# The attention score as three fp16 products in place of one fp32 product

## The chip, the cores and the metric

One core of a Trainium2 chip runs the whole program. The metric is the device time of that core in microseconds (us), the median of several runs. A core has TensorE (PE; its weight loads are PEld), VectorE (DVE), ScalarE (ACT), GpSimd (POOL, which does nothing here) and SyncE (SP, which issues the transfers). Each engine works through its own list of instructions in the order written; semaphores tie the lists together.

## The reference, cut to what matters

For 16 batches of 512 tokens with 512 features:

```
h   = gelu(x @ fc1_w.T + fc1_b)                       # 2048 hidden
x2  = x + concat(h @ fc2_w.T + fc2_b, h @ experts_w[idx].T + experts_b[idx])
att = tanh(x2 @ W1 + b1)                              # 128 values for each token
scores = att @ v                                      # one number for each token
out = x2 + softmax(scores under a prefix, postfix or all-but-own mask) @ x2 / count
```

The change touches `scores = att @ v` alone: a product of a 128-vector with a 128 x 512 tile per batch.

## The kernel before, in words

The tokens lie along the free dimension. A batch is one turn of the loop at L530 (82 us). All work of an engine is an order written out by hand, with a semaphore on each edge; nothing is planned by a program except that the VectorE list spreads the small steps of the pooling (`pool(n)`: the next n steps of the generator at L1172) between its other instructions.

**Split products.** Nearly all products are done as three fp16 products of a high and a low part: ScalarE writes the high part (`copy` with a scale, L622 and L623, as in `high`, L649), VectorE the low part (`low_part`, L1061 and L1062: value times scale minus high part), and TensorE adds weight-high x data-high, weight-high x data-low and weight-low x data-high. The scales are powers of two, found from a bound: a column of `mx` is summed over the partitions by TensorE (`chain_sum`, L274), and `chain_scale` (L1016) makes the scale `ex` and its inverse `ix` of it.

**The first layer** of a batch n is done in eight pairs of tiles, p = 0 to 7, by seven half-size products each (Strassen-like: `product1` to `product7`, L318 to L368, six 256-column matmuls each by `six`, L303). Between them VectorE adds halves in PSUM: `add_first` (L1107, its instruction is L1111) must be done before `product7` of that pair, and `add_second` (L1113, L1116) before `product4` and `product3`. ScalarE copies `product1` and `product5` (`copy_first`, `copy_fifth`) and does the gelu. Cycle c of L370 holds `product1(c)`, `product4(c-1)`, `product3(c-1)` and so on in steady order.

**The opening** (L433): at the end of batch b TensorE already starts pairs 0 and 1 of batch n = b + 1, mixed with the last expert products and the last chunk of the attention product, `attend(b, 3)`, whose two fp32 passes are L426. Then ScalarE does `tanh(b)` (L762, L769), from PSUM `pa` into `att`, TensorE does `score(b)` (L428, L431), and ScalarE keeps the result (`keep_score`, L771). The order around it:

```
TensorE  L444-449  attend(b,3) product7(n,0) product5(n,1) product6(n,1) product2(n,1) score(b)
         next      product4(n,0) product3(n,0) product1(n,2) product7(n,1) ...
ScalarE  L807-815  copy_first(n,1) tanh(b) copy_fifth(n,1) keep_score(b)
VectorE  L1453-57  add_first(n,0) add_second(n,0) pool(2) add_first(n,1) pool(3)
         L1393-06  pool(3) add_second(n,1) pool(1) add_first(n,2) low(n,0) pool(1) low(n,1) pool(1) add_second(n,2) ...
```

The stationary operand of the score is `avs`, the vector v repeated in 128 columns, so that every partition gets every score. `product1(n, 2)` writes the bank that holds the score and waits for `scored`. Batch 0 is done with simpler products (`tile`, L288) and a start-up of its own (L475 to L527); VectorE's part of it is L1365 to L1388. The last batch, 15, has its own end (L555 on), with `score_half` (L471) reading `avs` and `att` in two halves.

Of the kernel before, what the change touches and what calls it, by code (L numbers as in the profile page):

```python
# [35 lines left out]
def build(nc, xT, idx, pt, w1, b1, w2, b2, ew, eb, aw, ab, av, iota, ident, tokens, out):  # L36
# [4 lines left out]
    def sb(name, shape, dt=f32):  # L41
        return nc.alloc_sbuf_tensor(name, shape, dt)
# [20 lines left out]
    x2h = nc.alloc_sbuf_tensor_at("x2h", [P, S], f32r, offset=here())  # L63
    fifth = sb("fifth", [P, 2, HALF])
    aws_at = here()
    aws, avs = sb("aws", [P, KD, A]), sb("avs", [A, P])
    early_at = here()
    early = sb("early", [P, A])
    awl = [sb("awl0", [P, A], f32r), sb("awl1", [P, A], f32r),
# [17 lines left out]
    zFi, zFx = zF[:, 1:S + 1], zF[:, 0:S]  # L87
    zBx = zB[:, 1:S + 1]
    io = sb("io", [P, S], f16)
    b1s, b2s, ebs, abs_ = sb("b1s", [P, NH]), sb("b2s", [P, 3]), sb("ebs", [P, 2]), sb("abs", [P, 1])  # L90
    lcol, scol, shift, limit = sb("lcol", [P, 4]), sb("scol", [P, 4]), sb("shift", [P, 4]), sb("limit", [P, B])
    rz, ones = sb("rz", [P, 4]), sb("ones", [P, 1])
    idxs, pts = sb("idxs", [1, B], i32), sb("pts", [P, B], i32)
    ptf, e0, e1, e2 = (early[:, 64 + i * B:64 + (i + 1) * B] for i in range(4))
    cF, cS, cB, cntp, cntq, cD = (sb(n, [P, B]) for n in ("cF", "cS", "cB", "cntp", "cntq", "cD"))
# [1 line left out]


    oneb = sb("oneb", [P, P], bf16)
    NC = 17  # L100
    mx, ex, ix, lift = sb("mx", [P, NC], bf16), sb("ex", [P, NC]), sb("ix", [P, NC]), sb("lift", [P, NC])
    w1c, w2c = 3, 11

    def hc(b):
        return 14 * (b % 2)
# [7 lines left out]
    def scale_of(col):  # L113
        return ix[:, col:col + 1]
# [65 lines left out]
    def sem(name):  # L180
        return nc.alloc_semaphore("s_" + name)

    def sems(name, n):
# [2 lines left out]
                                       sems("ein", 2), sems("ebin", 2))  # L186
    (e0_in, idx_in, pt_in, b1_in, b2_in, aw_in, ab_in, av_in, io_in, eye_in, lcol_in) = (
        sem(n) for n in ("e0in", "idxin", "ptin", "b1in", "b2in", "awin", "abin", "avin", "ioin", "eyein", "lcolin"))

    (bits_set, summed, tile_done, p1, p5, p6, p7, p3, fc2_done, half_done, attended, score_done, nat_done, cols_done,  # L190
     totals_done, piece_done) = (sem(n) for n in (
# [78 lines left out]
    def tensor_program(eng):  # L270
# [3 lines left out]
        def chain_sum(n, lo, hi):  # L274

            if n > 1:
                e.wait_ge(pss_read, n - 1)
            mm(pss[:, lo:hi], oneb[:, :], mx[:, lo:hi], start=True, stop=True).then_inc(summed)
# [147 lines left out]
                mm(pa, aws[:, c, :], chunk(b, c), start=start, stop=stop).then_inc(attended)  # L426

        def score(b):  # L428
            e.wait_ge(tanh_done, b + 1)
            e.wait_ge(av_in, 16)  # L430
            mm(pa, avs[:, :], att, start=True, stop=True).then_inc(score_done)  # L431

        def opening(b):  # L433

# [35 lines left out]

        def score_half(v, n):  # L471
            e.wait_ge(tanh_done, LAST + 1 + v)
            mm(pf[n][:, 0:HALF], avs[:, :], att[:, HALVES[v]], start=True, stop=True).then_inc(score_done)


# [44 lines left out]
        attend(0, 0)  # L520
        fc2(0, 2, range(0, 4))
        e.wait_ge(bound_step, 6)
        chain_sum(9, hc(1), hc(1) + 3)
        fc2(0, 2, range(4, 16))
        attend(0, 1)
        fc2(0, 3, range(0, 12))
# [91 lines left out]
    def scalar_program(eng):  # L618
# [3 lines left out]
        def copy(o, x, scale=1.0):  # L622
            return act(o, x, ACT.Copy, scale=scale)  # L623
# [138 lines left out]
        def tanh(b):  # L762
            e.wait_ge(attended, nth_chunk(b, KD - 1))
            e.wait_ge(ab_in, 16)
            if b:
                e.wait_ge(score_done, b)
            else:
                e.wait_ge(sums_low_done, 2)
            act(att, pa, ACT.Tanh, bias=abs_[:, 0:1]).then_inc(tanh_done)  # L769

        def keep_score(b):  # L771
            e.wait_ge(score_done, b + 1)
            if b:
                e.wait_ge(pool_step, pool_value(b - 1, 11))
            else:
                e.wait_ge(sums_low_done, 1)
            copy(sc, pa).then_inc(scored)

        def exponentials(b, lo):
            e.wait_ge(pool_step, pool_value(b, 12))  # L780
# [91 lines left out]
        seed(0, 3)  # L872
        split_expert_high(0, 0)
        split_expert_high(0, 1)
        split_x_high(1, X11)
        split_x_high(1, T1)
        split_expert_high(0, 2)
# [118 lines left out]
    def vector_program(eng):  # L996
# [19 lines left out]
        def chain_scale(n, lo, hi):  # L1016

            e.wait_ge(summed, n)
            e.wait_ge(ones_set, 7)
            stt(ex[:, lo:hi], pss[:, lo:hi], TINY, lift[:, lo:hi], ALU.max, ALU.mult).then_inc(pss_read)  # L1020
            bits = ex[:, lo:hi].bitcast(i32)
            e.wait_ge(pss_read, n)
            ts(bits, bits, EXPONENT, None, ALU.bitwise_and).then_inc(ex_done)
            e.wait_ge(ex_done, n)
            eng.reciprocal(ix[:, lo:hi], ex[:, lo:hi]).then_inc(ix_done)
# [8 lines left out]
            ts(is2[:, b % 2, lo:hi], ix[:, col:col + hi - lo], ix[:, hc(b):hc(b) + 1], None, ALU.mult).then_inc(ds2_done)  # L1034

        def batch_scales(b):
            chain_scale(8 + b, hc(b), hc(b) + 3)
            fc1_scale(b, 8 + b, 0, PAIRS)
            out_scales(b, 8 + b, 3, 4, ec(b))
            out_scales(b, 8 + b, 0, 3, w2c)  # L1040
# [95 lines left out]
        def sums_low(p):  # L1136
            three, one = raw[:, p * 1024:p * 1024 + 768], raw[:, p * 1024 + 768:p * 1024 + 1024]
            c = scale_of(w1c + p)
            e.wait_ge(ones_high, p + 1)
            low_part(flat(w1l[:, 2 * p + 1, 0:2, :]), one, c, flat(w1h[:, 2 * p + 1, 0:2, :])).then_inc(sums_low_done)  # L1140
            e.wait_ge(three_high, p + 1)
            low_part(flat(cl[:, p, :, :]), three, c, flat(ch[:, p, :, :])).then_inc(sums_low_done)

        def pads():
            eng.memset(mF[:, 0:1], -BIG).then_inc(pads_set)
# [135 lines left out]
        eng.memset(ones[:, :], 1.0).then_inc(ones_set)  # L1281
        eng.memset(oneb[:, :], 1.0).then_inc(ones_set)
        eng.memset(x5[:, :, KD:KD + 1], 1.0).then_inc(ones_set)
        for lo, hi, power in ((0, 2, -14), (2, 11, -12), (11, 16, -14), (16, 17, -12)):
            eng.memset(lift[:, lo:hi], 2.0 ** power).then_inc(ones_set)
        w1_biggest(0)
        e.wait_ge(x_in[0], 16)
# [75 lines left out]
        for q in range(4):  # L1363
            w2_low(2, 0, q)
        weight_sums(0)  # L1365
        bounds(1)
        for p in range(4):
            sums_low(p)
# [2 lines left out]
        combine(1, T1)  # L1371
        combine(1, T2)
        expert_low(0, 1)
        pads()
        masks()
        combine(1, T3)
# [7 lines left out]
        weight_sums(4)  # L1384
        add_first(1, 0)
        add_second(1, 0)
        add_first(1, 1)
        sums_low(4)  # L1388


        for b in range(1, B):

            takes = ((0, 3, 1), (1, 1, 1), (1, 2, 1), (1, 2, 0), (1, 2, 0), (2, 2, 0))  # L1393
            if b == 1:
                takes = ((0, 0, 0),) * 5 + ((1, 1, 1),)
            for c, (one, two, three) in zip(range(2, PAIRS), takes):
                if c > 2:
                    low(b, 2 * c - 6)
                    pool(one)
                    low(b, 2 * c - 5)  # L1400
                pool(two)
                add_second(b, c - 1)
                pool(three)
                add_first(b, c)
                if b == 1 and 3 <= c < 6:
                    sums_low(c + 2)
            low(b, 10)
            pool(2 if b == 1 else 1)
            low(b, 11)
            pool(2 if b == 1 else 1)  # L1410
            add_second(b, PAIRS - 1)
            expert_low(b, 0)
            expert_low(b, 1)
            pool(2)
            low(b, 12)
            low(b, 13)
            expert_low(b, 2)
            expert_low(b, 3)
            low(b, 14)
            low(b, 15)  # L1420
            if b == LAST:
                break

            pool(1 if b == 1 else 2)
            if b == 1:
                for c in range(3):
                    e.wait_ge(awl_high, c + 1)
                    tt(awl[c][:, :], aws[:, c, :], awl[c][:, :].bitcast(f32), ALU.subtract).then_inc(awl_low)
            pool(3 if b == 1 else 4)
            bounds(b + 1)  # L1430
            pool(0 if b == 1 else 2)
            batch_scales(b + 1)
            for t in (T1, T2, T3, T4):
                combine(b + 1, t)
            pool(3)
            x2_low(b, 0)
            x_low(b + 1, X11)
            x_low(b + 1, T1)
            x_low(b + 1, T2)
            pool(3)  # L1440
            x_low(b + 1, X21)
            pool(2)
            x2_low(b, 1)
            x_low(b + 1, T3)
            x_low(b + 1, X22)
            pool(3)
            x_low(b + 1, T4)
            pool(3)
            x2_low(b, 2)
            pool(1)  # L1450
            pool(4)
            pool(3)
            add_first(b + 1, 0)  # L1453
            add_second(b + 1, 0)
            pool(2)
            add_first(b + 1, 1)
            pool(3)
# [70 lines left out]
    def sync_program(eng):  # L1528
# [35 lines left out]
        dma(b2s[:, :], b2).then_inc(b2_in, 16)  # L1564
        dma(pts[:, :], pt).then_inc(pt_in, 16)
        dma(abs_[:, :], ab).then_inc(ab_in, 16)
        dma(avs[:, :], av).then_inc(av_in, 16)
        dma(io[:, :], iota).then_inc(io_in, 16)
        dma(lcol[:, :], tokens).then_inc(lcol_in, 16)
        dma(aws[:, :, :], aw).then_inc(aw_in, 16)  # L1570
# [12 lines left out]
        for b in range(1, B):  # L1583
            if b < LAST:
                load_expert(b + 1)
            else:
                e.wait_ge(attended, nth_chunk(LAST - 1, 2))
                dma(aws[:, 0:3, :], aw[:, 0:3, :]).then_inc(aw_in, 16)
            if b > 1:
                for c in (1, 2, 3):  # L1590
                    store(b - 2, c)
            if b == LAST:
                e.wait_ge(el_done, nth_chunk(LAST, 3))
                dma(eye, ident).then_inc(eye_in, 16)
            store(b - 1, 0)
# [61 lines left out]
```

## Time and profile before

| | |
|---|---|
| time, median of 3 runs | 1362.59 us (1361.64 to 1362.98) |
| the profiled execution: its time | 1362.06 us |
| the profiled execution: its span, first to last instruction | 1360.3 us |
| busy in that span | TensorE 1348.4 us, VectorE 1231.0 us, ScalarE 868.7 us |
| mean granted TensorE clock | 0.999 of full speed |

The times in the rows are microseconds from the span's start; a duration without a unit is in us, "mean ns" is in nanoseconds. "Idle before" is the time in which the engine stood still ahead of these instructions, with what ended it. Matmuls are pipelined, so the distance between the starts of two of them, and not the duration of one, is what one costs in a stream.

### The profile page before, as it was taken

To read this page: it belongs to the slowest core of one execution; us is meant where nothing else is said; L and a number is where in the kernel's file an instruction comes from. 1 tells how busy PE (TensorE), PEld (TensorE's weight loads), DVE (VectorE), ACT (ScalarE), POOL (GpSimd) and SP (SyncE) were. 2 spreads that over 40 slices of the span, in tenths; PEclk is the share of its full clock that TensorE was granted. 3 is DMA by queue.
4 is the path that set the end of the run, shared out by engine and by line. 5 is a ranking of instruction groups with operands and counts; after the bars stand their busy time and mean duration, and the time that the engine had idled before them with its cause. 6 is when DMAs were issued, how large, how long until landed. Compare 5 with 4: busy or idle time off the path is not lost.

```text
span 1360.3 us, 22015 instructions
## 1 busy us (share of the span) xinstructions
PE 1348.4 (99%) x8734; PEld 869.8 (64%) x8734; DVE 1231.0 (90%) x2057; ACT 868.7 (64%) x1493; POOL 0.2 (0%) x4
## 2 busy tenths in 40 slices
PE   9999999999999999999999999999999999999998
PEld 4348476584766748567584765848567584765856
DVE  7896889899898998989899898998989999898998
ACT  4867848477583756838477483766838468483753
POOL 0000000000000000000000000000000000000000
PEclk9999999999999999999999999999999999999999
DMA  8410011110201102011020201102011020200001
GB/s 292 149 37 33 1 63 32 39 56 1 78 17 55 40 1 78 16 63 32 19 76 1 71 25 47 48 0 78 17 62 32 9 78 9 66 29 14 25 10 55
DMA packets 29192, 62.98 MB, mean 46 GB/s; under 512 B 5922, under 2 KB 6690, under 8 KB 26658
## 3 DMA queue, kind: packets, MB, share of 16 engines
q1 hardware_dynamic: 28658, 61.05, 13.8%
q8 instruction: 69, 1.13, 0.4%
q10 hardware_dynamic: 432, 0.53, 0.1%
q14 instruction: 33, 0.27, 0.1%
HBM read 44.79 MB, written 16.78 MB: 45 GB/s over the span
## 4 chain that ended last, share of the span: by engine, by line
PE 90%; DVE 7%; ACT 2%; DMA 1%; issue 0%; ACTq 0%; DVEq 0%
PE ps L394 14%; PE ps L396 14%; PE ps L395 14%; PE ps L313 13%; PE ps L314 13%; PE ps L315 13%; PE ps L284 1%; PE ps L431 1%; PE ps L426 1%; PE ps L596 1%; PE ps L422 1%; PE ps L421 1%; PE ps L420 1%; DVE hl L1062 1%; DMA er<-in_w 1%; DVE mx L1001 0%
## 5 line engine op out<-in xcount | busy, mean ns | idle before, releaser
L394 PE MATMUL ps<-hh,w2l 128*128 128x512 f16 x768 | 291.3, 379 | 0.7 <-ACT ps L623 0.7
L396 PE MATMUL ps<-hl,w2h 128*128 128x512 f16 x768 | 291.2, 379 | 0.0
L395 PE MATMUL ps<-hh,w2h 128*128 128x512 f16 x768 | 291.2, 379 | 0.0
L313 PE MATMUL ps<-xh,w1h 128*128 128x256 f16 x960 | 261.8, 273 | 0.0
L314 PE MATMUL ps<-xl,w1h 128*128 128x256 f16 x960 | 261.8, 273 | 0.0
L315 PE MATMUL ps<-xh,w1l 128*128 128x256 f16 x960 | 261.8, 273 | 0.0
L647 ACT ACTIVATE g<-ps,b1s,ds 128x512 f32<-128x512 f32 x240 | 173.5, 773 | 99.5 <-PE ps L315 98.5
L313 PE MATMUL ps<-xh,ch 128*128 128x256 f16 x720 | 196.4, 273 | 0.6 <-ACT ps L623 0.3
L315 PE MATMUL ps<-xh,cl 128*128 128x256 f16 x720 | 196.3, 273 | 0.0
L314 PE MATMUL ps<-xl,ch 128*128 128x256 f16 x720 | 196.3, 273 | 0.0
L1062 DVE SCALAR_TENSOR_TENSOR hl<-g,ix,hh 128x512 f16<-128x512 f32 x244 | 177.3, 739 | 1.6
L623 ACT ACTIVATE hh<-g,ix 128x512 f16<-128x512 f32 x244 | 162.1, 718 | 0.0
L396 PEld LDWEIGHTS ps<-hl,w2h 128*128 128x128 f16 x768 | 75.0, 98 | 90.8
L623 ACT ACTIVATE ps<-ps 128x256 f32<-128x256 f32 x120 | 44.6, 372 | 138.0 <-PE ps L315 138.0
L394 PEld LDWEIGHTS ps<-hh,w2l 128*128 128x128 f16 x768 | 74.9, 98 | 90.0 <-issue 4.3
L395 PEld LDWEIGHTS ps<-hh,w2h 128*128 128x128 f16 x768 | 75.0, 98 | 81.2 <-issue 0.7
L314 PEld LDWEIGHTS ps<-xl,w1h 128*128 128x128 f16 x960 | 93.8, 98 | 22.2 <-issue 5.0
L313 PEld LDWEIGHTS ps<-xh,w1h 128*128 128x128 f16 x960 | 93.9, 98 | 20.8 <-issue 3.6
L315 PEld LDWEIGHTS ps<-xh,w1l 128*128 128x128 f16 x960 | 93.9, 98 | 10.9
L394 PE MATMUL ps<-hh,el 128*128 128x512 f16 x240 | 91.3, 381 | 0.0
L395 PE MATMUL ps<-hh,eh 128*128 128x512 f16 x240 | 91.0, 379 | 0.0
L396 PE MATMUL ps<-hl,eh 128*128 128x512 f16 x240 | 91.0, 379 | 0.0
(208 smaller groups left out, 2343.3 us busy)
## 6 DMA issues: line engine op xcount, KB each, us to landing
xr<-in_xT SPq DMA_DIRECT2D x62, 256.0 KB, 3.1
er<-in_ew SPq DMA_DIRECT2D x15, 1024.0 KB, 5.6
out<-xr SPq DMA_DIRECT2D x60, 256.0 KB, 2.4
raw<-in_w SPq DMA_DIRECT2D x28, 256.0 KB, 6.2
er<-in_w SPq DMA_DIRECT2D x3, 1024.0 KB, 10.1
xr<-in_ew SPq DMA_DIRECT2D x1, 1024.0 KB, 5.7
out<-er SPq DMA_DIRECT2D x3, 256.0 KB, 2.5
xr<-in_xT ACTq DMA_DIRECT2D x2, 256.0 KB, 5.1
```

What stands on the lines that cost most here:

```text
L284: m = mm(pf[k % 4], w1r[k][:, c * P:(c + 1) * P], xr[:, 0, c, :], start=c == 0, stop=c == KD - 1)
L313: mm(to, wh, mh, start=i in (1, 5) and c == 0, stop=False, skip_group_check=True)
L314: mm(to, wh, ml, start=False, stop=False, skip_group_check=True)
L315: m = mm(to, wl, mh, start=False, stop=c == 1, skip_group_check=True)
L394: mm(po(b, o), wl, hh[:, k, :], start=False, stop=False, skip_group_check=True)
L395: mm(po(b, o), wh, hh[:, k, :], start=False, stop=False, skip_group_check=True)
L396: m = mm(po(b, o), wh, hl[:, k, :], start=False, stop=k == NH - 1, skip_group_check=True)
L420: mm(pa, awl[c][:, :], x2h[:, :], start=start, stop=False)
L421: mm(pa, awh[:, c, :], x2l[:, :], start=False, stop=False)
L623: return act(o, x, ACT.Copy, scale=scale)
L647: act(in_two(g_of(b, k)), src, ACT.Gelu, bias=b1s[:, k:k + 1], scale=ds1[:, b % 2, p:p + 1]).then_inc(gelu_done)
L1062: return stt(o, src, scale, hi, ALU.mult, ALU.subtract)
```

## The change

Batches 0 to 14 get their score from three fp16 products. `tanh` stays; ScalarE then copies `att` times 2^13 into `hh[:, 0, :]` (the slot of the hidden tile 0, which has been read by then) as fp16, and VectorE writes the low part into `hl[:, 0, :]` (`attention_low`). The vector v is loaded as one column (`vcol`), gets a scale like the weights (a new column `vc` = 17 of `mx`, `ex`, `ix`, summed along with the scales of batch 1), and `vh`, `vl` are its fp16 parts, repeated over 128 columns, in the place of `avs`. `keep_score` multiplies by `vinv`, which takes the scales out again. Batch 15 keeps the fp32 product; `avs` is loaded for it late.

```diff
@@ TensorE
         def score(b):
-            e.wait_ge(tanh_done, b + 1)
-            e.wait_ge(av_in, 16)
-            mm(pa, avs[:, :], att, start=True, stop=True).then_inc(score_done)
+            e.wait_ge(atth_done, b + 1)
+            e.wait_ge(vl_done, 1)
+            mm(pa, vl[:, :], hh[:, 0, :], start=True, stop=False)
+            mm(pa, vh[:, :], hh[:, 0, :], start=False, stop=False)
+            e.wait_ge(attl_done, b + 1)
+            mm(pa, vh[:, :], hl[:, 0, :], start=False, stop=True).then_inc(score_done)
...
         e.wait_ge(bound_step, 6)
-        chain_sum(9, hc(1), hc(1) + 3)
+        e.wait_ge(vmax_done, 1)
+        chain_sum(9, hc(1), vc + 1)
@@ ScalarE
             act(att, pa, ACT.Tanh, bias=abs_[:, 0:1]).then_inc(tanh_done)
+            e.wait_ge(tanh_done, b + 1)
+            copy(hh[:, 0, :], att, grow[:, 0:1]).then_inc(atth_done)
...
-            copy(sc, pa).then_inc(scored)
+            e.wait_ge(vinv_done, 1)
+            copy(sc, pa, vinv[:, 0:1]).then_inc(scored)
...
         split_expert_high(0, 1)
+        e.wait_ge(ix_done, 9)
+        copy(vh[:, :], vcol.broadcast_to([A, P]), scale_of(vc)).then_inc(vh_done)
         split_x_high(1, X11)
@@ VectorE
+        def attention_low(b):
+            e.wait_ge(atth_done, b + 1)
+            low_part(hl[:, 0, :], att, grow[:, 0:1], hh[:, 0, :]).then_inc(attl_done)
...
+        eng.memset(grow[:, :], 2.0 ** 13).then_inc(ones_set)
...
         weight_sums(0)
+        e.wait_ge(vcol_in, 16)
+        column(vc, vcol[:, :]).then_inc(vmax_done)
         bounds(1)
...
         expert_low(0, 1)
+        e.wait_ge(vh_done, 1)
+        low_part(vl[:, :], vcol.broadcast_to([A, P]), scale_of(vc), vh[:, :]).then_inc(vl_done)
+        ts(vinv[:, :], ex[:, vc:vc + 1], 2.0 ** -13, None, ALU.mult).then_inc(vinv_done)
         pads()
...
         add_second(1, 0)
+        attention_low(0)
         add_first(1, 1)
...
             add_second(b + 1, 0)
+            attention_low(b)
             pool(2)
             add_first(b + 1, 1)
@@ SyncE
-        dma(avs[:, :], av).then_inc(av_in, 16)
+        dma(vcol[:, :], av[:, 0:1], allow_slow_non_contiguous=True).then_inc(vcol_in, 16)
...
                 dma(aws[:, 0:3, :], aw[:, 0:3, :]).then_inc(aw_in, 16)
+                e.wait_ge(score_done, LAST)
+                dma(avs[:, :], av).then_inc(av_in, 16)
```

Beside this, the scales of batch 1 are taken over four columns in place of three, the small per-partition columns (`ones`, `abs_`, `rz`) move into one tile with the new ones, and `score_half` waits for `av_in`.

## Rows read from the trace of the kernel before

**Rows 1.** The page: busy time, and the chain that ended last, by engine.
```profile
PE 1348.4 (99%) x8734; PEld 869.8 (64%) x8734; DVE 1231.0 (90%) x2057; ACT 868.7 (64%) x1493; POOL 0.2 (0%) x4
...
PE 90%; DVE 7%; ACT 2%; DMA 1%; issue 0%; ACTq 0%; DVEq 0%
```

**Rows 2.** Timeline of TensorE, batch 4: start, duration, engine, line, operation, names.
```profile
428.75 0.38 PE L396 MATMUL ps<-hl,eh 128*128 128x512 f16 x1
428.97 0.38 PE L394 MATMUL ps<-hh,el 128*128 128x512 f16 x1
...
435.72 1.02 PE L431 MATMUL ps<-raw,avs 128*128 128x512 f32 x2
...
436.58 0.27 PE L313 MATMUL ps<-xh,w1h 128*128 128x256 f16 x1
```

**Rows 3.** Timeline of ScalarE in the same opening: tanh.
```profile
433.30 0.69 ACT L769 ACTIVATE raw<-ps,abs 128x512 f32<-128x512 f32 x1 [0.49 <-PE ps L426]
```

**Rows 4.** ScalarE by groups: mean ns of one, with and without a scale.
```profile
L623 ACT ACTIVATE hh<-g,ix 128x512 f16<-128x512 f32 x244 | 162.1, 718 | 0.0
L623 ACT ACTIVATE x2h<-xr 128x512 fp32r<-128x512 f32 x42 | 26.5, 631 | 58.1 <-PE ps L422 57.9
```

**Rows 5.** Timeline of VectorE, batch 4 to 5: first scan of the opening, add_second of pairs 1, 4, 6.
```profile
434.30 1.21 DVE L1253 TENSOR_TENSOR_SCAN raw<-raw 128x512 f32<-128x512 f32 x1
...
440.59 0.42 DVE L1116 TENSOR_TENSOR ps<-ps,fifth 128x256 f32<-128x256 f32 x1
...
441.86 0.74 DVE L1062 SCALAR_TENSOR_TENSOR hl<-g,ix,hh 128x512 f16<-128x512 f32 x1
442.51 1.22 DVE L1253 TENSOR_TENSOR_SCAN raw<-raw 128x512 f32<-128x512 f32 x1
...
454.73 0.41 DVE L1116 TENSOR_TENSOR ps<-ps,fifth 128x256 f32<-128x256 f32 x1
...
463.94 0.40 DVE L1116 TENSOR_TENSOR ps<-ps,fifth 128x256 f32<-128x256 f32 x1
```

**Rows 6.** Timeline of TensorE: the first matmul of product4 of pairs 1, 4, 6.
```profile
441.84 0.27 PE L313 MATMUL ps<-xh,w1h 128*128 128x256 f16 x1
...
455.60 0.27 PE L313 MATMUL ps<-xh,w1h 128*128 128x256 f16 x1
...
464.76 0.27 PE L313 MATMUL ps<-xh,w1h 128*128 128x256 f16 x1
```

**Rows 7.** Waits of VectorE, 434.2 to 480 us: us in total, times, longest.
```profile
DVE el L1062 <- ACT eh L623: 1.9, 2, 1.3
```

**Rows 8.** Timeline: TensorE held back by an add, and ScalarE by itself.
```profile
103.98 0.43 DVE L1111 TENSOR_TENSOR ps<-ps,fifth 128x256 f32<-128x256 f32 x1
104.55 0.27 PE L313 MATMUL ps<-xh,ch 128*128 128x256 f16 x1 [0.30 <-DVE ps L1111]
...
1315.12 0.72 ACT L947 ACTIVATE xr<-io,shift 128x512 f32<-128x512 f16 x1 [4.38 <-DVE shift L1481]
1315.88 0.72 ACT L949 ACTIVATE xr<-xr,limit 128x512 f32<-128x512 f32 x1
```

**Rows 9.** Timeline of the start-up and of the first opening.
```profile
79.84 0.47 DVE L1062 SCALAR_TENSOR_TENSOR w1l<-raw,ix,w1h 128x256 f16<-128x256 f32 x1
...
86.28 0.75 DVE L1062 SCALAR_TENSOR_TENSOR el<-xr,ix,eh 128x512 f16<-128x512 f32 x1 [0.72 <-ACT eh L623]
...
93.10 0.75 DVE L1062 SCALAR_TENSOR_TENSOR el<-xr,ix,eh 128x512 f16<-128x512 f32 x1
...
93.90 0.39 PE L394 MATMUL ps<-hh,el 128*128 128x512 f16 x1
...
106.71 0.43 DVE L1111 TENSOR_TENSOR ps<-ps,fifth 128x256 f32<-128x256 f32 x1 [0.88 <-PE ps L315]
```

**Rows 10.** The score's matmuls, first and last start; SyncE's timeline behind the last.
```profile
L431 PE MATMUL ps<-raw,avs x30: 592/594/595, 107.2 to 1256.4; 128*128 128x512 f32 x30
...
1260.35 23.14 SPq L1554 DMA_DIRECT2D out<-xr  x3
```

More of the change, by code:

```diff
@@ L65, in build @@
     aws_at = here()
-    aws, avs = sb("aws", [P, KD, A]), sb("avs", [A, P])
+    aws, avs_at = sb("aws", [P, KD, A]), here()
+    avs = sb("avs", [A, P])
+    vh, vl = (nc.alloc_sbuf_tensor_at(n, [A, P], f16, offset=avs_at + at) for n, at in (("vh", 0), ("vl", 2 * P)))
+    cols = sb("cols", [P, 16])
+    ones, abs_, vcol, vinv, grow, rz = (cols[:, lo:hi] for lo, hi in ((0, 1), (1, 2), (2, 3), (3, 4), (4, 5), (8, 12)))
     early_at = here()
@@ L89, in build @@
     io = sb("io", [P, S], f16)
-    b1s, b2s, ebs, abs_ = sb("b1s", [P, NH]), sb("b2s", [P, 3]), sb("ebs", [P, 2]), sb("abs", [P, 1])
+    b1s, b2s, ebs = sb("b1s", [P, NH]), sb("b2s", [P, 3]), sb("ebs", [P, 2])
     lcol, scol, shift, limit = sb("lcol", [P, 4]), sb("scol", [P, 4]), sb("shift", [P, 4]), sb("limit", [P, B])
-    rz, ones = sb("rz", [P, 4]), sb("ones", [P, 1])
     idxs, pts = sb("idxs", [1, B], i32), sb("pts", [P, B], i32)
@@ L99, in build @@
     oneb = sb("oneb", [P, P], bf16)
-    NC = 17
+    NC = 18
     mx, ex, ix, lift = sb("mx", [P, NC], bf16), sb("ex", [P, NC]), sb("ix", [P, NC]), sb("lift", [P, NC])
-    w1c, w2c = 3, 11
+    w1c, w2c, vc = 3, 11, 17
     def hc(b):
@@ L188, in build @@
         sem(n) for n in ("e0in", "idxin", "ptin", "b1in", "b2in", "awin", "abin", "avin", "ioin", "eyein", "lcolin"))
+    vcol_in, vmax_done, vh_done, vl_done, vinv_done, atth_done, attl_done = (
+        sem(n) for n in ("vcolin", "vmax", "vh", "vl", "vinv", "atth", "attl"))
     (bits_set, summed, tile_done, p1, p5, p6, p7, p3, fc2_done, half_done, attended, score_done, nat_done, cols_done,
@@ L472, in score_half @@
             e.wait_ge(tanh_done, LAST + 1 + v)
+            e.wait_ge(av_in, 16)
             mm(pf[n][:, 0:HALF], avs[:, :], att[:, HALVES[v]], start=True, stop=True).then_inc(score_done)
@@ L1018, in chain_scale @@
             e.wait_ge(summed, n)
-            e.wait_ge(ones_set, 7)
+            e.wait_ge(ones_set, 8)
             stt(ex[:, lo:hi], pss[:, lo:hi], TINY, lift[:, lo:hi], ALU.max, ALU.mult).then_inc(pss_read)
@@ L1036, in batch_scales @@
         def batch_scales(b):
-            chain_scale(8 + b, hc(b), hc(b) + 3)
+            chain_scale(8 + b, hc(b), hc(b) + 3 if b > 1 else vc + 1)
             fc1_scale(b, 8 + b, 0, PAIRS)
@@ L1283, in vector_program @@
         eng.memset(x5[:, :, KD:KD + 1], 1.0).then_inc(ones_set)
-        for lo, hi, power in ((0, 2, -14), (2, 11, -12), (11, 16, -14), (16, 17, -12)):
+        eng.memset(grow[:, :], 2.0 ** 13).then_inc(ones_set)
+        for lo, hi, power in ((0, 2, -14), (2, 11, -12), (11, 16, -14), (16, 18, -12)):
             eng.memset(lift[:, lo:hi], 2.0 ** power).then_inc(ones_set)
```

## The prediction

> **What bounds the kernel now.** I read the page first: TensorE is busy for 99% of the span and carries 90% of the chain that ended last; VectorE is busy for 90% [rows 1]. So a saving on TensorE should count in full, but VectorE has little room, and the question is where. That can't be read from an average. I then went to the timeline of one opening (batch 4 into 5, near 434 us), where the score lies, and from there followed VectorE until it next stood still. Openings repeat: the same adds lie at the same distances from the score at 190, 272 and 1256 us to within 0.02 us, so one stands for the 14 of batches 1 to 14.
>
> **TensorE's part.** The score starts at 435.72, and the next product at 436.58: the fp32 product takes 0.86 us of the stream. A 512-column fp16 matmul starts 0.22 us after the one before (more exactly 0.216; 0.86 is four of these) [rows 2]. Three take 0.65, so TensorE needs 0.21 us less per score, 15 x 0.21 = 3.2 us less in all. The Trainium skill (TensorE: Matmul & The Clock Gate, Back-to-back issue gap) says that in a real stream 512-column matmuls come every 131 ns or so; by it three would take 0.39 us and 15 scores would save 7 us. The stream here shows 216 ns, and I go by that.
>
> **What the new operands cost.** Tanh ends at 433.30 + 0.69 = 433.99 [rows 3]. An instruction of ScalarE that waits for its own predecessor starts 0.04 after that one's end (1315.12 + 0.72 to 1315.88) [rows 8], so the new copy starts at 434.03 and, at the 0.72 of a scaled fp16 copy [rows 4], ends at 434.75. VectorE starts some 0.04 later, 434.79, and its low part takes 0.74 like those of the hidden tiles, to 435.53 [rows 5]. TensorE wants it for the third product, at 435.72 + 0.43 = 436.15. So the score itself isn't held up; 0.6 us is left. The fifth copy, queued behind the new copy on ScalarE, now can't start before about 434.7; its reader on VectorE, `add_first` of pair 1, is queued behind two scans and comes later. `keep_score` gets a scale: an unscaled copy costs 631 and a scaled one 718 ns [rows 4], so it grows by about 0.08; the score ends 0.21 earlier. Only `product1` of pair 2 waits for it, and that lies two products behind the score, so this costs nothing.
>
> **What is queued behind the wait on VectorE.** This is the term that decides. Before, VectorE did `add_second` of pair 0 and went straight on with the pooling scan at 434.30 [rows 5]. Now `attention_low` stands between. It waits for the copy until 434.79, and the scan can start 0.65 after it (the distance from L1062 at 441.86 to the scan at 442.51) [rows 5], at 435.44: everything behind is 1.14 us later. Of this 0.65 is work and 0.49 is standing still. Is there a gap that takes it up? Between 434.2 and 480 VectorE waits only before the expert's low parts, 1.9 us in two pieces, the longer 1.3 [rows 7]; both come after the last add of pair 7. So VectorE runs through pairs 1 to 7 without a gap and stays 1.14 late through all of them.
>
> **Who waits for VectorE there.** `product4` of each pair needs `add_second`. TensorE held back by an add restarts 0.14 after its end (103.98 + 0.43 = 104.41 to 104.55) [rows 8]. The room in each pair is the start of `product4` minus the end of the add minus 0.14 [rows 5, 6]:
> - pair 1: 441.84 - 441.01 - 0.14 = 0.69;
> - pair 4: 455.60 - 455.14 - 0.14 = 0.32;
> - pair 6: 464.76 - 464.34 - 0.14 = 0.28.
>
> Pairs 2, 3, 5 and 7 have 0.45, 0.65, 0.61 and 0.89, and every `add_first` has 0.8 or more. TensorE has no idle time here and can't catch up later, so the tightest pair sets the result: it starts 1.14 - 0.28 = 0.86 us later than before, with the 0.21 saved already spent in waiting. The wait is taken in portions: 0.45 + 0.21 at pair 1, then 0.24 at pair 2, 0.13 at pair 4, 0.04 at pair 6. After pair 7 VectorE waits for ScalarE, which follows TensorE; its 1.3 us of idle time fall to about 1.0, and all engines are 0.86 late together. The rest of the batch (second layer, 35 us) moves as a block. The next opening starts with VectorE idle as before, and adds another 0.86. For 14 openings that is **+12.0 us**. Bounds per opening: below, the work alone without standing still and with a restart 0.10 faster, 0.65 - 0.38 = 0.27; above, the whole 1.14, if the rooms are worth nothing.
>
> **The first opening** differs: batch 1 spreads no pooling between its adds, so VectorE has gaps of about 1 us there (0.88 before the add at 106.71) [rows 9], and TensorE keeps its gain. After the score the chain goes over `keep_score` to ScalarE, where the scale costs 0.08: 0.13 gained of 0.21. **-0.1 us.**
>
> **Start-up.** VectorE bounds it from 88 to 104 us: TensorE's matmul at 93.90 comes right behind the low part that ends at 93.10 + 0.75 [rows 9], and that at 104.55 waits for an add [rows 8]. Into this run the change puts the low part of v. From 256 columns (0.47) and 512 (0.75) [rows 9], 128 columns give 0.34, or 0.26 start to start, and `vinv` adds 0.08: +0.34 us, seen in full at 93.90 and not again at 104.55. The maximum of v (0.1 to 0.2 us ahead of the bounds of batch 1) delays the sum for the scales, which TensorE waits for at 80; bounds 0 and 0.2, I take 0, since VectorE then stands 0.72 us waiting for ScalarE, at 86.28 [rows 9]. The copy of v on ScalarE (about 0.3) delays a split of x by less than that, and the split behind it waits for a difference from VectorE anyway. The memset and the load, now of one column, are covered by the wait for the first weights and by the 70 us before v is used. **+0.3 us**, bounds 0.1 and 0.7.
>
> **The end.** SyncE now waits for the score of batch 14 (its last pass started at 1256.4) before it loads `avs`; its next store was issued at 1260.35 anyway [rows 10], and the reader is some 70 us away. Nothing. The end is reached from pair 7 of batch 15 on, so all 14 shifts arrive in it.
>
> **Sum:** 12.0 - 0.1 + 0.3 = +12.2 us on the profiled execution's 1362.06: 1374.3. That execution lies 0.5 us under the median of 1362.59, so against the median the time is **1374.8 us**, 0.9% slower. A measurement of this kernel can tell about 0.2% (2.7 us) from no change.
>
> **Rivals.**
> 1. *The low part finds cover* (8%). TensorE's saving counts: 15 x 0.21 less 0.3, 1359.7 us. For it: TensorE is 99% busy and the room ahead of the score is 0.6 us. Against it: VectorE's delay would have to stay under 0.28 us, and its work alone is 0.65. Were the matmuls as fast as the Trainium skill's page has them, the same case would end near 1356; I give that 1% of the 8.
> 2. *Only part of the delay passes on* (14%): VectorE is late by its 0.65 of work, because the copy comes sooner or a pooling step shortens; 0.65 - 0.28 = 0.37 per opening, +5.2 + 0.2, 1368.0 us.
> 3. *The room in the pairs isn't there* (6%): the waits of TensorE and ScalarE feed back into the adds and the whole 1.14 counts, 14 x 1.14 + 0.2, 1378.8 us.
> 4. *Gain and delay cancel*, within 0.2% (3%): needs a delay near 0.4 us per opening.
>
> The forecast itself has 69%; its own errors (0.04 in the handovers, 0.1 in the durations, 14 times) make it 1372.5 to 1376.8. The range reaches down to rival 2 and short of rival 3: **1367.6 to 1378.0**. Faster 0.08, same 0.03, slower 0.89.
>
> **What would show it.** In the changed trace: the score takes 0.65 us of TensorE's stream; VectorE stands idle about 0.4 us before `attention_low`, 14 times; the scan after it starts 1.1 later relative to `attend`; TensorE waits for L1116's adds about 1.1 us per opening in three or four pieces, most of it before `product4` of pair 1; the period of a batch grows from 82.0 to 82.9; VectorE's idle time before the expert's low part shrinks by 0.3. I am wrong if TensorE shows no idle time before `product4`, or if that of pair 1 alone carries it.

## The result, and the profile after

Six executions of each kernel: 1361.97 us before (1361.64 to 1362.98), **1372.58 us after** (1372.37 to 1373.97). The ratio is 1.0078 with a 95% interval of 1.0068 to 1.0089: slower by 0.8%, as forecast in direction and nearly in size (+10.6 us, where the sum gave +12.2). The profiled execution of the kernel after took 1372.53 us with a span of 1370.8 us, 10.5 us more than the 1360.3 of before.

The page of the kernel after, its busy times and the chain by engine (compare [rows 1]):

```profile
PE 1352.9 (99%) x8749; PEld 866.8 (63%) x8749; DVE 1240.9 (91%) x2076; ACT 879.9 (64%) x1509; POOL 0.2 (0%) x4
...
PE 76%; DVE 17%; ACT 3%; issue 3%; DMA 1%; ACTq 0%; DVEq 0%
```

TensorE is still "99% busy", and the page's busy time has even grown, though it has less to do: busy shares don't show this slowdown. The chain does: VectorE's share went from 7% to 17%. TensorE's list of waits names the place. The first line is the wait of a matmul's weight load (PEld), the second that of the matmul itself, which is held by the same semaphore (us in total, times, longest):

```profile
PEld ps L318 <- DVE ps L1131: 22.9, 56, 0.7
...
PE ps L318 <- DVE ps L1131: 5.9, 14, 0.4
```

L318 is the first matmul of a half-size product (L313 of before) and L1131 is `add_second` (L1116 of before). Neither line was in the list before. 56 waits are four for each of 14 openings. The totals are not what was lost: idle time of a load counts here even where its matmul starts hardly late. The loss is read from the starts of the matmuls, below.

**The score.** TensorE's timeline in the opening of batch 4 (compare [rows 2]):

```profile
437.81 0.38 PE L436 MATMUL ps<-hh,vl 128*128 128x512 f16 x1
438.03 0.38 PE L437 MATMUL ps<-hh,vh 128*128 128x512 f16 x1
438.24 0.38 PE L439 MATMUL ps<-hl,vh 128*128 128x512 f16 x1
438.46 0.27 PE L318 MATMUL ps<-xh,w1h 128*128 128x256 f16 x1
```

From 437.81 to 438.46 are 0.65 us in place of 0.86, with no wait between the products. The saving on TensorE is there and is what was worked out. By the 131 ns in a stream that the Trainium skill gives (TensorE: Matmul & The Clock Gate, Back-to-back issue gap) the three would have taken 0.39 us, an estimate; this trace has 0.22 from start to start, and the measurement decides.

**The operands.** ScalarE's timeline of the same opening (compare [rows 3]):

```profile
435.39 0.69 ACT L779 ACTIVATE raw<-ps,cols 128x512 f32<-128x512 f32 x1 [0.49 <-PE ps L431]
436.11 0.72 ACT L633 ACTIVATE hh<-raw,cols 128x512 f16<-128x512 f32 x1
436.74 0.36 ACT L633 ACTIVATE fifth<-ps 128x256 f32<-128x256 f32 x1
438.66 0.69 ACT L633 ACTIVATE raw<-ps,cols 128x512 f32<-128x512 f32 x1 [1.55 <-PE ps L439]
```

And VectorE's, through the adds of pairs 1, 2, 4 and 6 (compare [rows 5]):

```profile
436.05 0.43 DVE L1131 TENSOR_TENSOR ps<-ps,fifth 128x256 f32<-128x256 f32 x1 [2.39 <-PE ps L320]
436.87 0.75 DVE L1077 SCALAR_TENSOR_TENSOR hl<-raw,cols,hh 128x512 f16<-128x512 f32 x1 [0.39 <-ACT hh L633]
437.54 1.22 DVE L1272 TENSOR_TENSOR_SCAN raw<-raw 128x512 f32<-128x512 f32 x1
...
443.83 0.42 DVE L1131 TENSOR_TENSOR ps<-ps,fifth 128x256 f32<-128x256 f32 x1
...
448.67 0.40 DVE L1131 TENSOR_TENSOR ps<-ps,fifth 128x256 f32<-128x256 f32 x1
...
457.96 0.41 DVE L1131 TENSOR_TENSOR ps<-ps,fifth 128x256 f32<-128x256 f32 x1
...
467.17 0.41 DVE L1131 TENSOR_TENSOR ps<-ps,fifth 128x256 f32<-128x256 f32 x1
```

Tanh starts 2.09 us later than before here (435.39 against 433.30: three openings of 0.78 us ahead of this one, less the 0.25 us by which batch 1 was early). Take 2.09 off: the scan is at 435.45 in place of 434.30, **1.15 us late** (forecast: 1.14), after 0.39 of standing still. The four adds are each 1.15 late too (443.83 - 2.09 - 440.59 = 1.15; the last one 467.17 - 2.09 - 463.94 = 1.14): nothing on VectorE took the delay up as far as pair 6. The next add, of pair 7, is only 0.91 late. These are the last add of pair 6, the low part behind it, and the add of pair 7, before and then after:

```profile
464.27 0.43 DVE L1111 TENSOR_TENSOR ps<-ps,fifth 128x256 f32<-128x256 f32 x1
464.81 0.75 DVE L1062 SCALAR_TENSOR_TENSOR hl<-g,ix,hh 128x512 f16<-128x512 f32 x1
...
467.86 0.42 DVE L1116 TENSOR_TENSOR ps<-ps,fifth 128x256 f32<-128x256 f32 x1
```

```profile
467.49 0.42 DVE L1126 TENSOR_TENSOR ps<-ps,fifth 128x256 f32<-128x256 f32 x1
467.82 0.74 DVE L1077 SCALAR_TENSOR_TENSOR hl<-g,ix,hh 128x512 f16<-128x512 f32 x1
...
470.86 0.42 DVE L1131 TENSOR_TENSOR ps<-ps,fifth 128x256 f32<-128x256 f32 x1
```

Before, the low part started 0.54 us after the add; after, 0.33. So there was a gap of 0.2 us that the list of waits [rows 7] doesn't show, and it swallowed 0.2 of the delay, though only behind pair 6, the pair that sets the result. The products that need the adds of pairs 1, 2, 4 and 6, on TensorE (compare [rows 6]):

```profile
444.31 0.28 PE L318 MATMUL ps<-xh,w1h 128*128 128x256 f16 x1 [0.42 <-DVE ps L1131]
...
449.13 0.28 PE L318 MATMUL ps<-xh,w1h 128*128 128x256 f16 x1
...
458.43 0.28 PE L318 MATMUL ps<-xh,w1h 128*128 128x256 f16 x1
...
467.64 0.28 PE L318 MATMUL ps<-xh,w1h 128*128 128x256 f16 x1
```

Each starts 0.06 us after the end of its add (443.83 + 0.42 = 444.25 to 444.31). Against before (pair 2 started at 446.43 there) they are late by 0.38, 0.61, 0.74 and 0.79 us, where 0.45, 0.69, 0.82 and 0.86 were forecast. So the delay comes in portions, at the pairs that were named; the first is 0.07 us smaller than forecast, and the others (0.23, 0.13, 0.05) are as forecast within 0.01. With the 0.21 spent at pair 1 TensorE loses 1.00 us to waiting in each opening (forecast: about 1.1).

ScalarE stands still more, too: in each of the 14 openings one gelu waits 1.2 us for a low part of VectorE (16.5 us in all). TensorE's list of waits has no line that such a gelu ended, so this isn't on the path.

**The period.** `attend(b, 3)` starts each opening's end and makes a good mark. The first and the last of batches 1 to 14, before, then after:

```profile
186.17 0.59 PE L426 MATMUL ps<-xr,aws 128*128 128x512 f32 x1
...
1252.50 0.59 PE L426 MATMUL ps<-xr,aws 128*128 128x512 f32 x1
```

```profile
185.92 0.59 PE L431 MATMUL ps<-xr,aws 128*128 128x512 f32 x1
...
1262.33 0.59 PE L431 MATMUL ps<-xr,aws 128*128 128x512 f32 x1
```

Over 13 batches that is 82.02 and 82.80 us per batch: **+0.78 us an opening**.

### The profile page after: what moved, and what is told of

The parts are those of the page before. It is cut to its first block, busy times and chain, and to the rows that moved or that the text cites. A ratio compares the mean times of both kernels' runs of the same rounds, so it can differ in the third digit from the quotient of the medians.

```text
span 1370.8 us, 22083 instructions
## 1 busy us (share of the span) xinstructions
PE 1352.9 (99%) x8749; PEld 866.8 (63%) x8749; DVE 1240.9 (91%) x2076; ACT 879.9 (64%) x1509; POOL 0.2 (0%) x4
## 4 chain that ended last, share of the span: by engine, by line
PE 76%; DVE 17%; ACT 3%; issue 3%; DMA 1%; ACTq 0%; DVEq 0%
PE ps L399 14%; PE ps L400 14%; PE ps L401 14%; PE ps L318 9%; PE ps L320 9%; PE ps L319 9%; DVE raw L1272 3%; DVE hl L1077 2%; DVE raw L1275 1%; ACT hh L633 1%; PE ps L289 1%; PE ps L431 1%; DVE ps L1131 1%; DVE xr L1289 1%; PE ps L606 1%
## 5 line engine op out<-in xcount | busy, mean ns | idle before, releaser
L318 PE MATMUL ps<-xh,w1h 128*128 128x256 f16 x960 | 262.2, 273 | 6.8 <-DVE ps L1131 5.9
L318 PE MATMUL ps<-xh,ch 128*128 128x256 f16 x720 | 196.4, 273 | 0.7 <-ACT ps L633 0.4
L1077 DVE SCALAR_TENSOR_TENSOR hl<-g,ix,hh 128x512 f16<-128x512 f32 x244 | 177.6, 740 | 0.1
L318 PEld LDWEIGHTS ps<-xh,w1h 128*128 128x128 f16 x960 | 93.8, 98 | 39.7 <-DVE ps L1131 22.9
L320 PEld LDWEIGHTS ps<-xh,w1l 128*128 128x128 f16 x960 | 93.9, 98 | 10.9
```

Source lines behind the costliest of these rows:

```text
L318: mm(to, wh, mh, start=i in (1, 5) and c == 0, stop=False, skip_group_check=True)
L320: m = mm(to, wl, mh, start=False, stop=c == 1, skip_group_check=True)
L1077: return stt(o, src, scale, hi, ALU.mult, ALU.subtract)
```

## The experiments

Theory: the change is slow because `attention_low` makes VectorE late, by its 0.65 us of work and by what it stands still ahead of it, and TensorE feels what exceeds the room before `product4` of pair 6. Rivals: the cost comes from ScalarE or from the fp16 products; the whole delay is passed on; work counts but standing still doesn't. In the table "period" is the same distance of marks, divided by 13. Each ratio is to executions of the kernel before that were made along with that run; their medians were 1361.97 us for e1 to e4, 1361.91 for e5, v1, v2 and c1, and 1362.13 for v3.

| kernel | time, median | ratio to before | period |
|---|---|---|---|
| before | 1361.97 | | 82.02 |
| after | 1372.58 | 1.0078 [1.0068, 1.0089] | 82.80 |
| e1, before with one more VectorE instruction | 1366.46 | 1.0032 [1.0020, 1.0044] | 82.33 |
| e2, before with two more | 1375.84 | 1.0103 [1.0087, 1.0118] | 83.00 |
| e3, after without the low part of tanh | 1357.07 | 0.9964 [0.9950, 0.9977] | 81.67 |
| e4, after with the scan first | 1366.44 | 1.0036 [1.0022, 1.0050] | 82.33 |
| e5, after with two waits on product4 | 1374.10 | 1.0090 [1.0076, 1.0104] | 82.89 |
| v1, after with two pooling steps moved | 1359.84 | 0.9988 [0.9979, 0.9997] | 81.79 |
| v2, scan first and one step moved | 1359.84 | 0.9986 [0.9977, 0.9995] | 81.88 |
| c1, before with the two steps moved | 1363.81 | 1.0012 [1.0003, 1.0021] | 82.02 |
| v3, v1 but for the last batch | 1360.65 | 0.9988 [0.9979, 0.9997] | 81.79 |

### e1 and e2: VectorE's time alone, in the kernel before

```diff
             add_second(b + 1, 0)
+            low_part(hl[:, 0, :], hl[:, 0, :], scale_of(hc(b)), hl[:, 0, :])
             pool(2)
```

e2 has a second one on `hl[:, 1, :]`.

> The kernel before with one more VectorE instruction in each of the openings 1 to 14, at the place of attention_low, but with no wait and no reader (its result lands in a slot that nobody reads any more). The score stays the fp32 product. Theory (VectorE's place in the queue is the whole cost, and the room in the tightest pair is what is left after a restart of 0.06 us: 464.76 - 464.34 - 0.06 = 0.36): the adds come 0.65 us later, 0.29 of it is seen, 14 x 0.29 = +4.1 us on before. Rival (the cost comes from the fp16 products, the copy on ScalarE or the wait, not from VectorE's time): no change. Rival (the whole delay is passed on): +9.1 us.

> The same with two such instructions per opening, 1.30 us of VectorE's time and no wait. Theory: 1.30 - 0.36 = 0.94 us per opening, +13.2 us on before, so the second instruction costs its full length while the first cost less than half. Rival (not VectorE): no change. Rival (whole delay passed on): +18.2 us.

Measured: +4.5 and +13.9 us. Some of the executions had a slightly lower mean granted clock (0.999 in place of 1.000; two of the six of e1, two of the four of e2, two of the ten of before) and were over 1 us longer; by the medians of those at 1.000 it is +4.3 and +13.2, where +4.1 and +13.2 were expected. The first instruction takes 0.66 us of VectorE's list and lengthens the period by 0.31, the second lengthens it by 0.66, its full time. That is the signature of a room that is used up once: 0.66 - 0.31 = 0.35, where the rows give 0.36. These kernels have no fp16 product for the score, no new copy and no new wait, so VectorE's lateness is enough to make TensorE late.

### e3: no low part

```diff
             mm(pa, vl[:, :], hh[:, 0, :], start=True, stop=False)
-            mm(pa, vh[:, :], hh[:, 0, :], start=False, stop=False)
-            e.wait_ge(attl_done, b + 1)
-            mm(pa, vh[:, :], hl[:, 0, :], start=False, stop=True).then_inc(score_done)
+            mm(pa, vh[:, :], hh[:, 0, :], start=False, stop=True).then_inc(score_done)
...
-            attention_low(b)
```

> The kernel after without attention_low and without the third product of the score, so the low part of the tanh is left out; the copy on ScalarE, the scaled keep_score and the start-up work stay. Theory (VectorE alone makes the change slow): VectorE isn't late, TensorE needs 0.86 - 0.43 = 0.43 us less per score, 15 x 0.43 = 6.4 us less than before, with the start-up some 0.1 to 0.3 us more: 0.995 of before, about 1355.8 us. Rival (ScalarE's copy or the scaled keep_score holds something up): slower than before, or at least not faster by more than 3 us.

Measured: 4.9 us faster than before. The copy on ScalarE, the scaled `keep_score` and the start-up are all in it, so none of these makes the change slow. It fell short of the 6.4 expected: the period shrank by 0.36 and not by 0.43. The list of waits between 130 and 1250 us shows where:

```profile
PEld ps L318 <- DVE ps L1129: 4.7, 13, 0.4
```

L1129 is `add_second` again, one wait in each batch (the 4.7 us are idle time of the load, of which only 0.07 a batch is lost). VectorE's list isn't faster than in the kernel before, so TensorE can only run ahead by the room of 0.36; the other 0.07 is spent waiting for the add of pair 6. That is 1.0 of the missing 1.5 us. The room is a limit on a gain as well as on a delay.

### e4: work against standing still

```diff
             add_second(b + 1, 0)
-            attention_low(b)
-            pool(2)
+            pool(1)
+            attention_low(b)
+            pool(1)
```

> The kernel after with attention_low behind the first scan of the pooling in place of ahead of it (batches 1 to 14). The scan fills the time in which VectorE stood waiting for the copy. Theory: VectorE is 0.65 late in place of 1.15, and 0.29 of it is seen per opening; the third product of the score waits about 0.1 us, which is taken up in the same 0.29. 14 x (0.78 - 0.29) = 6.9 us faster than after, about 4 us slower than before: 1366 us. Rival (the work on VectorE counts, the standing still doesn't): no change against after, 1372.6 us.

Measured: 6.1 us faster than after, 4.5 slower than before. VectorE's timeline of one opening of e4:

```profile
434.63 0.43 DVE L1131 TENSOR_TENSOR ps<-ps,fifth 128x256 f32<-128x256 f32 x1 [2.39 <-PE ps L320]
434.98 1.21 DVE L1272 TENSOR_TENSOR_SCAN raw<-raw 128x512 f32<-128x512 f32 x1
436.11 0.73 DVE L1077 SCALAR_TENSOR_TENSOR hl<-raw,cols,hh 128x512 f16<-128x512 f32 x1
436.75 1.22 DVE L1275 TENSOR_TENSOR_SCAN raw<-raw 128x512 f32<-128x512 f32 x1
```

No idle time is left ahead of L1077, and the period is that of e1 (82.33), which has the same work and no wait either. So of the 0.78 us an opening, 0.47 was the standing still. (The third product of the score starts 0.06 us late here, 0.28 behind the second in place of 0.22; the period shows none of it.)

### e5: how fast TensorE restarts

The row on which I had priced the restart (0.14 us, [rows 8]) didn't hold in the pairs (0.06). The start-up matmul has two waits ahead of it.

```diff
         def product4(b, p):
-            e.wait_ge(xl_done, nth_x(b, T4))
+            eng.wait_ge(xl_done, nth_x(b, T4))
             e.wait_ge(added1, nth_pair(b, p))
```

(`eng` writes the wait each time, where `e` leaves it out if the value has been reached.)

> The kernel after with a second wait, on x's low part, which has long been done, ahead of every product4, so that the wait for add_second isn't the only one in front of that matmul. In the kernel after, TensorE restarts 0.06 us after the end of the add where it waits for it alone; the 0.14 of the start-up row is a matmul with two waits ahead of it. Theory (the number of waits makes the difference): restarts after 0.14, so the room is 0.28 and each opening costs 0.08 more, 14 x 0.08 = +1.1 us on after, 1373.7 us. Rival (the start-up row is slow for another reason): restarts after 0.06, no change.

Measured: the period grew by 0.09, the time by 1.5 us. The first product4 that waits:

```profile
444.52 0.27 PE L318 MATMUL ps<-xh,w1h 128*128 128x256 f16 x1 [0.51 <-DVE ps L1131]
```

Its add ended at 443.95 + 0.42 = 444.37: the restart takes 0.15, and 0.14 to 0.16 at nearly all of the other waits in the 14 openings. A second wait, though long fulfilled, costs 0.09 us here where the other one holds; at the product4 that don't wait the period shows no cost.

### v1, v2, c1 and v3: giving the delay a place

Two pooling steps of 0.60 us each leave the stretch without gaps and go behind the bounds of the next batch, where VectorE waits for TensorE's sum, and on to its wait in the opening. v1:

```diff
             expert_low(b, 1)
-            pool(2)
+            pool(4 if b == LAST else 2)
...
             bounds(b + 1)
-            pool(0 if b == 1 else 2)
+            pool(0 if b == 1 else 4)
...
             add_first(b + 1, 1)
-            pool(3)
+            pool(1)
```

> The kernel after with two of VectorE's pooling steps (0.60 us each) taken out of the stretch from the opening to pair 7 and put behind the bounds of the next batch (in the last batch, ahead of the low part of hidden tile 12). Theory: VectorE is 1.15 - 1.20 us late in the pairs, so no add holds TensorE back, and the 0.21 us per score is seen at last: 15 x 0.21 less 0.3 for the start-up (whose own scatter is about 0.4) = 2.9 us faster than before, 1359 us, and 13.5 us faster than after. Rival (the second half of the batch has no room either and the delay comes up there, at the sum for the scales or at the low parts of x2): between before and after, 1363 to 1370 us.

> The kernel after with attention_low behind the first scan and one pooling step moved to behind the bounds. Theory: VectorE is 0.65 - 0.60 late; the third product waits about 0.1 us of the 0.21 gained, so 14 x 0.12 + 0.1 less 0.3 = 1.5 us faster than before, about 1360.5 us. Rival (standing still doesn't count, work does): as v1.

c1 makes v1's edit in the kernel before:

> The kernel before with the same two pooling steps moved as in v1 and nothing else. Theory: TensorE wasn't held back by VectorE in the pairs, so giving VectorE more room there changes nothing: within 0.1% of before. Rival (v1 is faster because of the moved steps alone): as fast as v1, 3 us faster than before.

v1 and v2 are the first kernels with all three products to come out under both kernels, 12.7 us under the kernel after but only 0.12 and 0.14% under the one before. That is less than the 0.2% that the prediction took as what can be told; the intervals exclude 1 by little, and it is the period that says it plainly. In v1's period of 81.79 the whole 0.21 is seen (0.23). v2 keeps 0.15, since the third product waits for its operand. Its matmul starts 0.27 us behind the second one in place of 0.22; the load's row counts 5.0 us in 13 openings, of which the period shows 0.08 us an opening as lost:

```profile
PEld ps L439 <- DVE hl L1077: 5.0, 13, 0.4
```

c1 came out slower than expected, by 1.9 us, and the expectation of no change was wrong; but its period is exactly that of before, 82.02. So the steps moved are worth nothing by themselves in the 13 regular batches, and the loss lies behind the mark of batch 14: 110.0 us to the end against 107.8. There VectorE's list from the expert's low parts on is on the path, and I had put the two steps into it: from 1294 us on each of its instructions is 1.0 us late against that mark, and TensorE has a new wait of 0.7 us for a low part there, in c1 as in v1. The rest, in the profiled execution, is TensorE's clock behind the wait for the last exponentials (stretch; its length, then busy time of PE, PEld, DVE, ACT, POOL; granted clock, DMA share, GB/s):

```profile
1340.00:1345.00 5.00, 3.03 (x15) 1.21 (x13) 4.89 (x8) 2.74 (x5) 0.00 (x0) 1.00 0.00 0
1345.00:1350.00 5.00, 5.00 (x18) 4.19 (x19) 4.60 (x8) 4.32 (x7) 0.00 (x0) 0.66 0.00 0
```

0.66 is a stretch partly at 1.2 and partly at 2.4 GHz. The other executions agree with this split: the five of c1 with a mean clock of 1.000 have a median of 1363.11 us, 1.2 us above those of before, so about 1.2 of the 1.9 us is the moved steps. v3 therefore spares the last batch (`attention_low` behind the first scan and no step moved in the opening into it):

> v1 (the kernel after with two pooling steps moved behind the bounds), but the opening into the last batch moves no step and has attention_low behind the first scan. In the last batch VectorE's list from the expert's low parts to the end is itself on the path, and c1 and v1 ended 0.8 to 1.0 us later there in VectorE's list. Theory: batches 2 to 14 keep the 0.23 us that each gained in v1, the last one costs the 0.3 of e4: 0.5 us faster than v1 in the profile's span, 1357.4 against 1357.9 us, and 0.998 of before. Rival (the last batch's delay came from elsewhere): as v1.

It wasn't faster than v1: 1358.0 against 1357.9 us of span, and a median of 1360.65 against 1359.84. From the last mark it took 108.3 in place of 108.5 us, but its start-up happened to be 0.3 longer, and 8 of its 11 executions had the lower mean clock, against 4 of 11 of v1. Its three at 1.000 (1359.21 to 1359.75) overlap with the seven of v1 (1359.30 to 1360.17). A gain of 0.2 us there is below what these runs can tell.

## Why the prediction was right, point by point

- **The place.** Right: TensorE waits before `product4` for `add_second`, in four portions, in each of 14 openings, and e1 and e2 show that VectorE's time alone does it.
- **VectorE's delay.** Forecast 1.14, measured 1.15; the 0.49 of standing still in it is real (0.47 by e4). That VectorE has no gap through pairs 1 to 7 holds only to pair 6: behind it 0.2 us was taken up. It cost the forecast nothing, since pair 6 is the tightest, but one of the signs failed by it: VectorE's idle time ahead of the expert's low part fell from 1.30 to 1.19 us, by 0.11 in place of 0.3.
- **TensorE's saving.** 0.21 us, measured 0.21, and not seen in the end time, since it is spent in the wait at pair 1.
- **The room.** Here the sum was off: 0.28 by a restart of 0.14, in truth 0.36 by a restart of 0.06. That is 0.08 in each of 14 openings, 1.1 of the 1.7 us by which the sum was too high. I took the restart from the one row in which TensorE waited for an add, and that matmul had two waits ahead of it (e5). The term was mis-sized; the mechanism stood. 14 x 0.78 = 10.9 us in place of 12.0. Of the rest, 0.4 is the start-up and 0.1 the last batch.
- **First opening.** From the mark of batch 0 (103.22, after: 103.10) to that of batch 1 it is 82.95 before and 82.82 after: -0.13, as worked out.
- **Start-up.** Forecast +0.3. The score of batch 0 came 0.13 *earlier*. The new instructions did cost what was said. These are VectorE's rows after, the maximum of v, its low part and `vinv`:

```profile
78.64 0.15 DVE L1016 TENSOR_REDUCE mx<-cols 128x1 bf16<-128x1 f32 x1
...
89.74 0.34 DVE L1077 SCALAR_TENSOR_TENSOR vl<-cols,ix,vh 128x128 f16<-128x128 f32 x1
90.01 0.14 DVE L1398 TENSOR_SCALAR cols<-ex 128x1 f32<-128x1 f32 x1
```

  The maximum delayed the sum for the scales, which TensorE does near 79.6 us, by 0.07 (forecast: 0), and the low part and `vinv` delayed the matmul near 93.8 by 0.27: together +0.34 us. Against it stand 0.46 us by which the third weight block was summed sooner in this execution (67.58 against 68.04), so that the forecast of +0.3 was right and isn't seen. The 0.46 is taken as scatter and not as the smaller load: the same sum came at 67.36 in e2, with the loads of before, and at 67.97 in e3, with the new ones.
- **The end.** No cost, as said; the last batch took 0.67 more than before behind its mark, where 0.78 was due by the period.
- **Rivals.** None came about. That the low part finds cover needed a delay under the room; e1 and e4 show that even the work alone exceeds it. Rival 2, a delay of the work alone, is what e4 built; in the change itself VectorE stood still for 0.39 us in each opening. Rival 3, the whole delay, is ruled out by the period (0.78, not 1.14) and by e1. Rival 4 needed a delay near 0.4.

The scatter of 1 to 2 us between executions of one kernel goes with the clock. In v1 the seven executions with a mean granted clock of 1.000 took 1359.30 to 1360.17 us, the four with 0.999 took 1361.07 to 1361.51; e1, e2, e4 and v2 part in the same way, before, c1 and v3 less cleanly. The profiles of e1, v2 and c1 show where, in the last 20 us; those of before, after, e2 to e5, v1 and v3 show no lower clock while TensorE still had work. Whether it is the same place in the executions without a profile, and why it happens in some and not in others, stays open.

## What to carry to other kernels

A saving on the busiest engine can be lost, and more than lost, if its operands are made on an engine whose list has no gap in the next 30 us. Look not for that engine's busy share but for the smallest distance between one of its results and the instruction that takes it, over the whole stretch until it next stands still. What a new instruction cost here was its work plus the time its engine stood waiting ahead of it, less that smallest room, each time. The same room capped what the busy engine could gain. So put a new wait behind work that can be done meanwhile, and move work of no urgency to the other side of the next gap.

## What the runs showed of the hardware that I had not expected

A matmul held by one wait started 0.06 us after the end of the VectorE instruction that it waited for; with a second wait ahead of it, fulfilled long before, it took 0.15. And TensorE's granted clock fell to half (1.2 GHz) in some executions in the last 20 us, shortly behind TensorE's wait for the last exponentials. In c1 TensorE had waited 1.97 us, and the clock was at 0.50 to 0.70 from 1345 to 1349 us. In v1 it had waited 1.97 us too, and was busy for the same 3.03 us of the stretch from 1340 to 1345 us, and the clock stayed at 1.00. Likewise e1 and before both waited 1.81 us there, and only e1 fell. What TensorE did just before doesn't tell these apart.
